# Cross attention: the groups of four that share value tiles begin at the third batch, their splits are spread over eight steps, and the fourth batch's units sit at other steps

## What is computed

```python
x = layernorm(x + self_attention(x))             # causal, relu scores with a distance factor
x = layernorm(x + cross_attention(x, ctx, ctx))  # the part that changes
x = layernorm(x + ffn(x))                        # 512 -> 1536 gated -> 512

# cross attention, for each batch
q = (query @ Wq.T + bq).reshape(100, 16, 32)
k = (ctx @ Wk.T + bk).reshape(722, 16, 32)
v = (ctx @ Wv.T + bv).reshape(722, 16, 32)
probs = softmax(einsum('qhd,khd->hqk', q / sqrt(32), k))
out = einsum('hqk,khd->qhd', probs, v) @ Wo.T + bo
```

## Time and profile before

| | |
|---|---|
| median of 3 runs | 2466.43 us (2465.69 to 2467.71) |
| the profiled execution's own time | 2464.95 us |
| its span, first to last instruction | 2463.2 us |
| mean granted TensorE clock | 0.984 |
| PE busy | 2366.3 us, 96% of the span |
| DVE, ACT, POOL busy | 62%, 54%, 55% |
| cross attention's steps on PE | about 536 to 1950 us |

### The profile page before, as it was taken

One profiled execution on the slowest core, in us unless ns is written; L12 is line 12 of the kernel. 1 busy time (PEld: TensorE's weight loads), 2 busy tenths in 40 slices (PEclk: granted clock), 3 DMA queues, 4 the chain that ended last, 5 costly groups with the idle time before them and its releaser, 6 DMA issues.

```text
span 2463.2 us, 58715 instructions
## 1 busy us (share of the span) xinstructions
PE 2366.3 (96%) x21644; PEld 2051.5 (83%) x21644; DVE 1535.1 (62%) x2621; ACT 1331.4 (54%) x3301; POOL 1361.6 (55%) x1189
## 2 busy tenths in 40 slices
PE   7999978989999999999999999999999899999999
PEld 7887847887888888888888888888888698998998
DVE  6666678835667666667666667666666725335342
ACT  5777762115666666666666666666666651221311
POOL 5677563327575675676666666765665533333332
PEclk9999969999999999999999999999999999999999
DMA  7776777624676776776776766766766841101010
GB/s 227 198 226 179 199 187 264 250 92 132 190 208 188 185 201 187 198 198 189 191 194 187 205 192 186 199 190 187 199 188 190 232 146 65 39 26 63 1 39 23
DMA packets 293198, 408.91 MB, mean 166 GB/s; under 512 B 148540, under 2 KB 168508, under 8 KB 292924
## 3 DMA queue, kind: packets, MB, share of 16 engines
q1 hardware_dynamic: 268348, 354.96, 50.4%
q10 hardware_dynamic: 24576, 50.36, 8.1%
HBM read 138.81 MB, written 52.43 MB: 78 GB/s over the span
## 4 chain that ended last, share of the span: by engine, by line
PE 63%; issue 5%; POOL 5%; DVE 2%; ACT 1%; DMA 1%; SPq 1%; ACTq 1%; POOLq 0%; DVEq 0%
PE D_ps_p L68 33%; PE D_ps_s L1862 6%; PE E_ps_g L68 5%; PE E_ps_u L68 5%; PE E_ps_d L68 5%; PE D_ps_p L1889 5%; PE E_ps_y L68 3%; POOL D_e L1398 2%; POOL D_ctx_low L1413 1%; ACT D_e L1532 1%; DVE D_columns L1667 1%; DVE D_turned L1681 1%; SPq L1286 1%; POOL D_ctx_high L1411 1%; ACTq L1548 1%
## 5 line engine op out<-in xcount | busy, mean ns | idle before, releaser
L1398 POOL TENSOR_SCALAR D_e<-D_e,D_columns 128x722 f32<-128x722 f32 x256 | 538.3, 2103 | 485.0 <-DVE D_columns L1673 484.9
L1532 ACT ACTIVATE D_e<-D_ps_s,D_columns 128x723 f32<-128x723 f32 x512 | 437.7, 861 | 390.1 <-DVE D_columns L1667 341.8
L1667 DVE TENSOR_REDUCE D_columns<-D_ps_s 128x1 f32<-128x723 f32 x512 | 439.5, 899 | 292.2 <-PE D_ps_s L1862 292.1
L1681 DVE STREAM_TRANSPOSE D_turned<-D_e 128x768 f32<-128x768 f32 x512 | 496.0, 972 | 26.0 <-DMA D_pT<-D_turned 17.4
L68 PE MATMUL D_ps_p<-D_ctx_high,cross_wk_high 128*128 128x362 f32 (+1 forms) x1024 | 350.8, 343 | 8.0 <-POOL D_ctx_low L1413 5.3
L68 PE MATMUL D_ps_p<-D_ctx_low,cross_wk_high 128*128 128x362 f32 (+1 forms) x1024 | 337.4, 330 | 0.0
L68 PE MATMUL D_ps_p<-D_ctx_high,cross_wk_low 128*128 128x362 f32 (+1 forms) x1024 | 335.7, 328 | 0.0
L68 PE MATMUL D_ps_p<-cross_wv_high,D_ctx_high 128*128 128x512 f32 (+1 forms) x656 | 260.0, 396 | 0.0
L68 PE MATMUL D_ps_p<-cross_wv_high,D_ctx_low 128*128 128x512 f32 (+1 forms) x656 | 259.3, 395 | 0.0
L68 PE MATMUL D_ps_p<-cross_wv_low,D_ctx_high 128*128 128x512 f32 (+1 forms) x656 | 257.9, 393 | 0.0
L1539 ACT ACTIVATE D_e<-D_e,D_columns 128x722 f32<-128x722 f32 x256 | 230.9, 902 | 14.6 <-DVE D_columns L1673 14.3
(11 more groups left out here) (230 smaller groups left out, 5268.7 us busy)
## 6 DMA issues: line engine op xcount, KB each, us to landing
D_pT<-D_turned SPq DMA_DIRECT2D x1536, 96.0 KB, 2.6
D_pT<-D_turned ACTq DMA_DIRECT2D x512, 96.0 KB, 2.7
D_craw<-in_ctxT SPq DMA_DIRECT2D x124, 361.0 KB, 3.9
self_q<-A_q_out SPq DMA_DIRECT2D x10, 640.0 KB, 4.1
self_k<-A_k_out SPq DMA_DIRECT2D x10, 640.0 KB, 3.9
self_v<-A_v_out SPq DMA_DIRECT2D x25, 256.0 KB, 3.6
A_q<-self_q SPq DMA_DIRECT2D x32, 200.0 KB, 3.7
A_k<-self_k SPq DMA_DIRECT2D x32, 200.0 KB, 4.4
```

The costliest lines, as they stand in the source:

```text
L1398: pool.tensor_scalar(head, head, inv[:, 2 * (s % 2):2 * (s % 2) + 1], None, ALU.mult)\
L1532: act.activation(e[n // 2 % 2][:, n % 2, 0:PARTS * PART].rearrange("p (a c) -> p a c", a=PARTS), parts_of(n), ACT.Exp, bias=neg_max[:, n % ...
L1667: dve.tensor_reduce(neg_max[:, n % 4:n % 4 + 1], parts_of(n), AX.XY, ALU.max, negate=True)\
L1681: dve.transpose(turned[quad % 2][:, :, 2 * (s % 2) + h, :].rearrange("p j (t r) -> p t j r", r=32), e[s % 2][:, h, :].rearrange("p (t j r) ...
```

## The change

The groups of four now cover batches 2 to 29 (`FOURS = (B - 2) // 4`, seven groups as before), so the fourth batches are 5, 9, ..., 29, and batches 0, 1, 30 and 31 share nothing. The counts of units, copies and splits stay the same: seven fourth batches with five value units each.

The five units of a fourth batch are set by `FOURTH_V_STEP = (5, 7, 8, 9, 11)` in place of the first five of `V_STEP`, 5, 6, 7, 9, 10.

The split of the combined tiles is made in eight half steps, cast and subtract apart, at `TAIL_STEP = (-2, 1, 2, 3, 6, 6, 9, 9)` counted from the first step of batch `4q + 1`, and behind the step's pieces. Before, each of four steps, at `8 * (4q - 1)` and the three after it, held a cast and a subtract, ahead of the pieces. `load_tails` stands one batch later in SP's order, and the first one behind the loads of batch 1's last two context pieces.

```diff
--- before.py
+++ after.py
@@ -993,7 +993,10 @@
     QB = T // BLOCKS
     RUN = ST * 32
 
-    SHARED = B - 4
+
+    FOURS = (B - 2) // 4
+    FOURTH_V_STEP = (5, 7, 8, 9, 11)
+    TAIL_STEP = (-2, 1, 2, 3, 6, 6, 9, 9)
     FULL = S - LAST
     THIRD = 32
     STEPS = PAIRS * B
@@ -1132,26 +1135,30 @@
 
             return moved[quad % QUADS]
 
+        def of_four(b):
+            return (b - 2) // 4, (b - 2) % 4 if 2 <= b < 4 * FOURS + 2 else None
+
         def is_fourth(b):
-            return b < SHARED and b % 4 == 3
+            return of_four(b)[1] == 3
 
         def shares(b):
-            return b < SHARED and b % 4 < 3
+            return of_four(b)[1] in (0, 1, 2)
 
         def values_taken(b, n=None):
 
-            taken = 26 * (min(b, SHARED) // 4) + 7 * (b % 4) if b < SHARED else 26 * (SHARED // 4) + ST * (b - SHARED)
+            taken = sum(ST + shares(a) - is_fourth(a) for a in range(b))
             return taken + (0 if n is None else n + 1 + (shares(b) and n == ST - 1))
 
         unit_at, sum_at, piece_at, queries_at, tail_at = {}, {}, {}, {}, {}
-        for q in range(SHARED // 4):
-            for k in range(KD):
-                tail_at[PAIRS * (4 * q - 1) + k + (2 if q == 0 else 0)] = (q, k)
+        for q in range(FOURS):
+            for i in range(2 * KD):
+                tail_at.setdefault(PAIRS * (4 * q + 1) + TAIL_STEP[i], []).append((q, i // 2, i % 2))
         for b in range(B):
             for u in range(KU):
                 unit_at.setdefault(PAIRS * (b - 1) + u + 2, []).append(("k", b, u))
             for i in range(ST - is_fourth(b)):
-                unit_at.setdefault(PAIRS * (b - 1) + V_STEP[i], []).append(("v", b, i))
+                step = FOURTH_V_STEP[i] if is_fourth(b) else V_STEP[i]
+                unit_at.setdefault(PAIRS * (b - 1) + step, []).append(("v", b, i))
             for m in range(QUADS):
                 sum_at[PAIRS * b + 2 * m + SUM_AFTER] = QUADS * b + m
                 queries_at[PAIRS * (b - 1) + QUERY_STEP[m]] = (b, m)
@@ -1262,12 +1269,12 @@
                 def load_tails(q):
                     wait(sp, t_low, KD * q)
                     for i in range(3):
-                        sp.dma_start(tails_raw[:, :, i * P:i * P + LAST], c_rows[4 * q + i, :, :, FULL:S])\
+                        sp.dma_start(tails_raw[:, :, i * P:i * P + LAST], c_rows[4 * q + 2 + i, :, :, FULL:S])\
                           .then_inc(t_loaded, 16)
                     for i in range(3):
                         first, end = FULL + THIRD * i, min(FULL + THIRD * (i + 1), S)
                         sp.dma_start(tails_raw[:, :, (i + 1) * P - THIRD:(i + 1) * P - THIRD + end - first],
-                                     c_rows[4 * q + 3, :, :, first:end]).then_inc(t_loaded, 16)
+                                     c_rows[4 * q + 5, :, :, first:end]).then_inc(t_loaded, 16)
 
                 def load_q(b):
                     wait(sp, q_done, QUADS * b)
@@ -1327,10 +1334,10 @@
                 load_ctx(1, 1)
                 sp.wait_ge(q_stored, 64 * NG)
                 load_q(0)
+                load_ctx(1, 2)
+                load_ctx(1, 3)
                 sp.wait_ge(t_clear, 1)
                 load_tails(0)
-                load_ctx(1, 2)
-                load_ctx(1, 3)
                 for b in range(B - 1):
                     load_q(b + 1)
                     if b > 0:
@@ -1343,8 +1350,8 @@
                         store(b - 1)
                     if b + 2 == B:
                         load_first_outputs()
-                    if b % 4 == 2 and b + 2 < SHARED:
-                        load_tails((b + 2) // 4)
+                    if b % 4 == 3 and (b + 1) // 4 < FOURS:
+                        load_tails((b + 1) // 4)
                     move(QUADS * b + 1)
                     if b + 2 < B:
                         load_ctx(b + 2, 2)
@@ -1413,14 +1420,16 @@
                     pool.tensor_tensor(cs[b % 2][1][:, k, :], craw[k % 2][:, :],
                                        cs[b % 2][0][:, k, :].bitcast(F32), ALU.subtract).then_inc(c_low, 1)
 
-                def split_tails(q, k):
-                    if k == 0:
-                        wait(pool, u_done, unit_count["v", 4 * q - 2, ST - 1] if q else 0)
+                def split_tails(q, k, low):
+                    if k == 0 and not low:
+                        wait(pool, u_done, unit_count["v", 4 * q, ST - 1] if q else 0)
                         pool.wait_ge(t_loaded, 96 * (q + 1))
-                    pool.tensor_copy(tails[0][:, k, :], tails_raw[:, k, :]).then_inc(t_high, 1)
-                    pool.wait_ge(t_high, KD * q + k + 1)
-                    pool.tensor_tensor(tails[1][:, k, :], tails_raw[:, k, :], tails[0][:, k, :].bitcast(F32),
-                                       ALU.subtract).then_inc(t_low, 1)
+                    if not low:
+                        pool.tensor_copy(tails[0][:, k, :], tails_raw[:, k, :]).then_inc(t_high, 1)
+                    else:
+                        pool.wait_ge(t_high, KD * q + k + 1)
+                        pool.tensor_tensor(tails[1][:, k, :], tails_raw[:, k, :], tails[0][:, k, :].bitcast(F32),
+                                           ALU.subtract).then_inc(t_low, 1)
 
                 last = QUADS * B - 1
 
@@ -1479,10 +1488,10 @@
                         normalise_first(s)
                     if s in queries_at:
                         block_queries(*queries_at[s])
-                    if s in tail_at:
-                        split_tails(*tail_at[s])
                     for b, k in piece_at.get(s, []):
                         split_piece(b, k)
+                    for q, k, low in tail_at.get(s, []):
+                        split_tails(q, k, low)
                     if s >= MAIN - 2:
                         for k in range(2):
                             low_of(acts, acts_raw, o_high, 2 * (s - MAIN + 2) + k, o_low)
@@ -1521,9 +1530,10 @@
                         wait(act, pv_done, QUADS * (b - 1))
                     act.activation(vs[b % 2][0:rows, i, :], bank("v", b, i)[0:rows, 0:D], ACT.Copy).then_inc(v_done, 1)
                     if shares(b) and i == ST - 1:
-                        first = THIRD * (b % 4)
+                        q, j = of_four(b)
+                        first = THIRD * j
                         size = min(THIRD, LAST - first)
-                        act.activation(fourth[b // 4 % 2][first:first + size, :],
+                        act.activation(fourth[q % 2][first:first + size, :],
                                        bank("v", b, i)[P - THIRD:P - THIRD + size, 0:D], ACT.Copy).then_inc(v_done, 1)
 
                 def exps(n):
@@ -1839,9 +1849,10 @@
                     rows = P if i < ST - 1 else LAST
                     wait_bank(pe, "v", b, i)
                     if shares(b) and i == ST - 1:
-                        pe.wait_ge(t_low, KD * (b // 4 + 1))
+                        pe.wait_ge(t_low, KD * (of_four(b)[0] + 1))
+                        place = slice(of_four(b)[1] * P, of_four(b)[1] * P + P)
                         products(pe, bank("v", b, i)[:, 0:D], SPLIT, KD,
-                                 lambda a, k: tails[a][:, k, b % 4 * P:(b % 4 + 1) * P],
+                                 lambda a, k: tails[a][:, k, place],
                                  lambda a, k: W[1][a][:, k, :]).then_inc(u_done, 1)
                         return
                     products(pe, bank("v", b, i)[0:rows, 0:D], SPLIT, KD,
@@ -1883,7 +1894,7 @@
                     wait_bank(pe, "o", quad, 0)
                     out = bank("o", quad, 0)
                     for i in range(ST):
-                        values = fourth[b // 4 % 2] if is_fourth(b) and i == ST - 1 else vs[b % 2][:, i, :]
+                        values = fourth[of_four(b)[0] % 2] if is_fourth(b) and i == ST - 1 else vs[b % 2][:, i, :]
                         for j in range(4):
                             c = m * P + j * HD
                             last = pe.matmul(out[HD * j:HD * (j + 1), 0:T], values[:, c:c + HD],
```

## The result

The changed kernel takes 2449.31 us (median of 6 runs, 2447.53 to 2453.41) against 2466.06 us before (6 runs): a ratio of 0.9935, 95% interval 0.9922 to 0.9947. The prediction was 2449.4 us. That the two agree to 0.1 us is luck: the six runs of the changed kernel alone spread over 5.9 us. The profiled execution has a span of 2446.1 us, 17.1 less than the one of before.

What follows compares the result with a forecast made beforehand. PE, busy 96% of the span, was taken as the bound, with only idle time and clock to gain: 9.9 (middle) + 5.0 (start) + 2.2 (clock) = 17.1 us, 2466.43 - 17.1 = 2449.4 us; range 2445.5 to 2459.5.

Steps and rivals of the forecast that it cites:

- The bound: Middle of cross attention: PE's work is fixed, and its 9.93 us of idle time is the most to gain there.
- The fourth batch's units: Slot 1 of fourth batches: no lone even-step unit delays ACT's odd exponentials; seven late slots fall to 9.60 us, gain 9.9.
- Two short slots in a row: Slots 2 and 3 before the fourth batch, and its slots 1 and 2: delays carried over taken as nothing.
- the bound of 1.37 us a slot: Upper bound on the cost of each new short slot, the stall that the trace shows.
- SP: Batches 3, 7, ..., 23: tails' DMAs make a slot 3 turn late by up to 2.39 us, costing nothing with two units.
- The splits' new places: Middle, POOL: PE waits for no split; without cover, up to 1.5 us in each of seven groups.
- The start: Second to third scores: piece 3 split at 567.8, not 572.8, gaining 5.0 us; full clock for 48 matmuls gains 2.2.
- The gap ahead of the first subtract: POOL behind the reduction: 7.52 us, taken as bound to the first subtract, whichever it is, so moving to piece 0.
- The alternative of the prediction: POOL at the start: a built-in subtract owes nothing, the gap is the tails' own; the sum larger by 0.2 us.
- Only the middle: Rival, 2456.5 us: at the start something else holds PE as long, such as a piece's load; chance 0.08.
- only the start: Rival, 2459.3 us: one new short slot in each group waits instead, 1.37 us each; chance 0.09.
- Slower: Rival, 2478 us: 21 short slots stall in the middle at 1.37 us each as turns wait for moves; chance 0.05.

Runs made afterwards that it cites:

- e3: The kernel before with only the last value unit of each fourth batch moved, from step 10 to 11; 2456.16 us, ratio 0.9962 to before.
- e4: The kernel before with ACT taking the fourth batch's lone even-step value unit after the next step's two exponentials; 2453.62 us, ratio 0.9960 to before.
- e9: The changed kernel with the fourth batches' units at 5, 6, 8, 9, 10, so two lone even-step units a group; 2469.29 us, ratio 1.0017 to before.
- e1: The kernel before with only the fourth batches' units moved to 5, 7, 8, 9, 11; 2455.94 us, ratio 0.9965 to before.
- e12: The changed kernel with the tails' loads one batch later, in batches 4, 8, ..., 24, where slot 3 is short; 2447.29 us, ratio 0.9921 to before.
- e5: The changed kernel with the tails' splits packed again at steps 0 to 3 of the fourth batch, ahead of the pieces; 2447.54 us, ratio 0.9938 to before.
- e7: The changed kernel with a subtract of one column right behind the reduction on POOL; 2447.57 us, one run.
- e6: The kernel before with POOL's partition_all_reduce replaced by a copy; 2460.20 us, ratio 0.9980 to before.
- e2: The changed kernel with the fourth batches' units back at 5, 6, 7, 9, 10; 2458.63 us, ratio 0.9976 to before.
- e10: The changed kernel with four cast and subtract pairs put back on POOL at steps -6 to -3; 2455.23 us, ratio 0.9956 to before.

## Why the prediction was right

- **The bound.** PE's work is fixed and its idle time is what can be saved. Before, 9.93 us of idle time in the middle, 9.62 of it in the seven slots; after, 0.31. These 0.31 us are a wait in the slot of quad 2, in both kernels. The prediction counted them as gain and said that every slot from quad 2 on takes 9.55 us or more; quad 2's own takes 9.01, and the rule holds from quad 3 on. Nothing else rests on that.
- **The fourth batch's units: 9.9 us forecast, 10.3 measured in the middle.** Of the 10.3 us, 9.6 are idle time and 0.7 are busy time of PE, 1307.00 against 1306.30 us for the same matmuls, which the prediction took as fixed. e3 gets it by moving one unit, e4 by moving ACT's copy alone, and e9 doubles the cost by a second lone unit. That ACT's order behind a lone unit at the even step is the cause is shown.
- **Two short slots in a row** hold, as taken, at 9.6 us; the bound of 1.37 us a slot wasn't needed. Three in a row hold too (e3).
- **SP.** That the tails' load costs nothing where slot 3 has two units, and would find less cover in a short one, is borne out: in the changed kernel turns wait up to 2.52 us for moves in two-unit slots and PE loses nothing, while in e1 and e12 eleven of twelve loads at a short slot cost 0.3 to 0.7 us. The slack of about 2 us was well sized, for a wait of 1.67 us cost nothing and one of 2.08 us did. But the price came by a way that the prediction had not worked out. It named DVE's slack to the next maximum; what runs out first is ACT's normalisation and the copy behind it, which hold a bank that PE wants.
- **The splits' new places: nothing forecast, nothing measured** (e5).
- **The start: 7.2 us forecast, 7.45 measured.** The chain was nearly right. It had piece 3 split at 567.8; the piece was done at 567.18 in a profile whose first `scores` stands 0.7 us later, so 1.3 us sooner against PE. Of that, 0.6 us are the load of piece 2, which came in 3.3 us after its issue (556.88, cast at 560.14) and not 3.9; 0.5 are the gap, 7.06 us and not 7.52; and most of the rest is that the reduction stood only 0.3 us later. So PE does not idle for the 0.25 us that the sum left it. The clock's part is as forecast: the 48 matmuls run at 1.00.
- **The gap ahead of the first subtract.** The choice to bind it to that subtract, wherever it stands, was right (changed kernel, e7), and e6 shows that it comes with the reduction. The alternative of the prediction, that a built-in subtract owes nothing, does not hold here: the first one behind the reduction has 6.6 to 7.8 us ahead of it. The Trainium skill (GPSIMD Engine Reference, section 2.1, Instruction dispatch) gives about 6 us for the first call to a freshly loaded kernel, and the 5.6 to 6.6 us ahead of the reduction in the twelve profiles that have one agree. It doesn't say that a built-in subtract is free behind such a call; that was the prediction's own reading of it.
- **The rivals.** None came. *Only the middle* is e3's or e4's kernel, 2456.16 and 2453.62 us against 2456.5 forecast; *only the start* is e2's, 2458.63 against 2459.3. *Slower* needed short slots that stall, and its nearest relative, e9, is slower than before by a ratio of 1.0017.
- **The sum.** 17.1 us were forecast. The two places together gave 17.8, and in the two profiles the first `scores` stands 0.7 us later in the changed kernel, for which no run gives a reason and which is within the spread of that time from run to run. So the terms were right, and the last tenth of a microsecond was luck.

The two parts of the gain don't depend on each other: e2's start (11.19 us) and e3's middle (1309.76 us) are those of the changed kernel, and the ratios say the same within their intervals (0.24% and 0.38% against 0.65%). Most of what stays idle in cross attention lies in batch 31, whose first three slots take 10.7, 10.2 and 11.4 us in the changed kernel, with waits of `scores` for ACT of 0.36 and 1.77 us; the change leaves that, and no run here was aimed at it.

## What to carry to other kernels

In a pipeline where in-order engines walk through the same steps, look for the one step whose producer stands early and whose consumer's queue holds something urgent behind it: here a copy of 0.6 us, waiting for its matmuls ahead of an exponential, cost 1.4 us each time, and either the producer one step later or the copy behind the next two exponentials removes it. When a unit of work is left out of a regular pattern, the place of the hole matters as much as its size. And count what stands on the queue that everyone waits for at a stage's start, one-off instructions and the gaps around them included: taking away either 6 us of splits that could wait or one reduction freed PE of 5 us of idle time and of 2 us more at the low clock.

## What the runs showed of the hardware that wasn't expected

- The `partition_all_reduce` on POOL took 0.38 us in itself, with 5.6 to 6.6 us of gap ahead of it and 6.6 to 7.8 us ahead of the first `tensor_tensor` behind it (twelve profiles), while copies and casts between the two ran at their usual speed to within 0.1 us. At the start of each gap the trace has a pair of `MODIFY_POOL_CONFIG`. Without the reduction (e6) neither gap nor pair was there.
- Behind 5.25 us of idle time PE's granted clock was 0.50, its low level (1.2 GHz), from 572.83 to 577.00 us, and 1.00 (2.4 GHz) from 578 us on; the 48 matmuls took 11.92 us. Behind 3.94 us of idle time they took 12.01 (e10). Behind none they ran at 1.00 throughout. In the middle, the stops of 1.33 to 1.54 us of the kernel before left the clock at 1.00.
